# q, k and V of an attention block moved by DMA: transposes for q and k, a way through DRAM for V

## The reference

```python
U, _ = jnp.linalg.qr(P)                       # 288 x 64
R = expm(skew(silu(cond) @ W.T + b))          # 2 x 64 x 64
z = jnp.einsum('btn,nd->btd', x, U)
x = x + jnp.einsum('btd,nd->btn', jnp.einsum('btd,bde->bte', z, R) - z, U)
ada = jax.nn.silu(c) @ ada_w + ada_b          # shift, scale, gate, twice
def attention(x):
    qkv = (x @ qkv_w + qkv_b).reshape(n, t, 3, H, DH)
    q, k, v = qkv[:, :, 0], qkv[:, :, 1], qkv[:, :, 2]
    attn = jnp.einsum('nthd,ntkd->nthk', q * DH ** -0.5, k)   # of one token, head against head
    out = jnp.einsum('nthk,ntkd->nthd', jax.nn.softmax(attn, -1), v)
    return out.transpose(0, 2, 1, 3).reshape(n, t, d) @ proj_w + proj_b
x = x + gate_msa * attention(modulate(layernorm(x), shift_msa, scale_msa))
x = x + gate_mlp * (gelu(modulate(layernorm(x), shift_mlp, scale_mlp) @ fc1_w + fc1_b) @ fc2_w + fc2_b)
```

## Time and profile before

| | |
|---|---|
| median of 3 runs | 427.33 us (426.06 to 427.52) |
| profiled execution, first to last instruction | 422.3 us |
| median less that span | 5.0 us |
| busy TensorE | 397.1 us |
| busy VectorE | 291.1 us |
| busy ScalarE | 231.8 us |
| busy GpSimd | 115.9 us |
| mean granted TensorE clock, share of full | 0.987 |

### The profile page before, as it was taken

How to read it: one execution, slowest core, us unless ns; L and a number is a source line. 1 busy time by engine, 2 the same in 40 slices (tenths; PEclk the granted TensorE clock), 3 DMA queues, 4 the chain that set the end, 5 groups by cost and what they waited for, 6 DMA issues and landing times.

```text
span 422.3 us, 11278 instructions
## 1 busy us (share of the span) xinstructions
PE 397.1 (94%) x4547; PEld 256.5 (61%) x4547; DVE 291.1 (69%) x793; ACT 231.8 (55%) x485; POOL 115.9 (27%) x137
## 2 busy tenths in 40 slices
PE   8999999999989899899978898889999999999996
PEld 4656555666545566666646565558755566666675
DVE  2688875677689856667757766666899776746452
ACT  3356334433257899997786785665775342422100
POOL 5039999981008700000000000005420010101040
PEclk9999989999989999999999999999999999999999
DMA  6999000000000000000000000000000000000011
GB/s 166 305 316 271 24 4 2 12 7 2 2 0 2 2 2 3 2 2 5 2 4 3 5 4 4 4 2 2 0 2 1 16 28 16 23 20 16 29 43 42
DMA packets 7926, 14.68 MB, mean 35 GB/s; under 512 B 2555, under 2 KB 6239, under 8 KB 7748
## 3 DMA queue, kind: packets, MB, share of 16 engines
q1 hardware_dynamic: 7874, 13.96, 11.0%
HBM read 11.52 MB, written 2.38 MB: 33 GB/s over the span
## 4 chain that ended last, share of the span: by engine, by line
PE 71%; DVE 14%; ACT 10%; issue 4%; ACTq 0%; DVEq 0%
PE psum L957 13%; PE psum L973 13%; PE psum L517 9%; PE psum L803 6%; ACT scratch L1068 3%; PE psum L787 2%; PE psum L880 2%; PE psum L617 2%; DVE MX L1373 2%; ACT big L1101 2%; PE psum L934 2%; PE psum L629 2%; PE psum L751 2%; PE psum L573 2%; PE psum L608 2%
## 5 line engine op out<-in xcount | busy, mean ns | idle before, releaser
L957 PE MATMUL psum<-scratch,W 128*128 128x512 f16 (+1 forms) x252 | 57.9, 379 | 0.0
L973 PE MATMUL psum<-W,big 128*128 128x288 f16 x432 | 55.1, 286 | 0.0
L506 POOL TENSOR_TENSOR X<-X,big 128x288 f32<-128x288 f32 x16 | 13.0, 826 | 150.0 <-ACT big L1174 149.7
L803 PE MATMUL psum<-WQ,scratch 128*128 128x288 f16 (+1 forms) x336 | 50.5, 294 | 2.8 <-DVE scratch L1368 1.9
L1199 ACT ACTIVATE big<-psum 128x512 f32<-128x512 f32 x36 | 21.3, 597 | 57.3 <-PE psum L957 52.3
L973 PEld LDWEIGHTS psum<-W,big 128*128 128x128 f16 x432 | 42.2, 98 | 12.9
L1373 DVE TENSOR_REDUCE MX<-psum 128x8 f32<-128x1024 f32 x32 | 39.0, 1220 | 11.4 <-PE psum L751 11.0
L517 PE MATMUL psum<-ident 128*32 128x192 f32 (+3 forms) x142 | 43.8, 393 | 0.0
L1129 ACT ACTIVATE big<-psum 128x1024 f32<-128x1024 f32 x32 | 32.9, 1032 | 15.0 <-PE psum L843 14.7
L957 PEld LDWEIGHTS psum<-scratch,W 128*128 128x128 f16 (+1 forms) x252 | 24.6, 98 | 25.6
L803 PEld LDWEIGHTS psum<-WQ,scratch 128*128 128x128 f16 (+1 forms) x336 | 30.6, 100 | 14.8 <-DVE scratch L1368 2.4
(11 more groups left out here) (221 smaller groups left out, 770.5 us busy)
## 6 DMA issues: line engine op xcount, KB each, us to landing
X<-in_x_dram SPq DMA_DIRECT2D x4, 576.0 KB, 14.8
out_dram<-big SPq DMA_DIRECT2D x16, 144.0 KB, 1.7
big<-in_L_cond_W_dram SPq DMA_DIRECT2D x1, 2268.0 KB
big<-in_L_cond_ada_w_dram SPq DMA_DIRECT2D x2, 864.0 KB, 18.2
stage<-in_L_cond_fc_w_dram SPq DMA_DIRECT2D x1, 1296.0 KB, 18.9
big<-in_L_cond_fc_w_dram SPq DMA_DIRECT2D x1, 1152.0 KB
stage<-in_L_cond_qkv_w_dram SPq DMA_DIRECT2D x1, 864.0 KB
big<-in_L_cond_fc_w_dram SPq DMA_DIRECT2D x3, 144.0 KB
```

The costliest lines, as they stand in the source:

```text
L803: mm = pe.matmul(UB[gu % 2][:, 0:D], HT[0:r, n % 2, a_, P * a:P * a + P], WQ[0:r, w_, D * w:D * w + D], start=(p_ == 0), stop=(p_ == 6))
L957: mm = pe.matmul(FB[idx % 3], W1[0:r, w_, P * m:P * m + P], HT[0:r, n % 2, a_, :], start=(p_ == 0), stop=(p_ == 6))
L973: mm = pe.matmul(YB[t % 2][:, 0:D], g[:, a_, f, cols], W2[:, w_, f, :], start=(f == 0 and a_ + w_ == 0), stop=(f == NF - 1 and w_ == 1))
```

## The change

q and k are no longer turned on TensorE. SP issues one DMA transpose for each of q and k of a pair (16 in all), from `HQ`, which now holds two pairs with both tiles of a head side by side, into `QKT`. The columns come out in the order of tokens, so `operand` reads them with a step of 16. The row of maxima is no longer turned on TensorE either: ScalarE scales `MX` into `MRT`, and SP writes it with four DMAs. V goes from PSUM to `SV` by one ScalarE copy a tile, from there by SP into a DRAM tensor, and GpSimd's own queue reads it back in the form that `values` needs, with eight DMAs a pair, into one of six buffers. Buffers 0 to 3 lie in `big`, where `VT` was, 4 and 5 in `scratch`. GpSimd clears the buffers and sets their column of ones. The projections rotate through three banks in place of two.

```diff
+        values_d = nc.dram_tensor("value_rows", [2 * NCH, 8, 2, 16, D], F32, kind="Internal").ap()
...
-        UB, CB = [bank[2], bank[5]], [bank[6], bank[7]]
+        UB = [bank[2], bank[5], bank[6]]
...
         def operand(s_, c_, w, g, rows):
             b, u = divmod(s_, 16)
-            return QKT[b][R * c_:R * c_ + rows, w, P * (4 * u + g):P * (4 * u + g + 1)]
+            pr, v = divmod(4 * u + g, 16)
+            cols = QKT[b][R * c_:R * c_ + rows, w, 16 * P * pr:16 * P * (pr + 1)]
+            return cols.rearrange("p (t v) -> p v t", v=16)[:, v]
...
+            def store_values(pr, c_):
+                k = 2 * pr + c_
+                sp.wait_ge(v_copied, k + 1)
+                sp.dma_start(values_d[pr, :, c_], SV[:, k % 4, :]).then_inc(v_stored[k % 4], 16)
+
+            def turn_heads(pr, w):
+                if pr == NCH and w == 0:
+                    sp.wait_ge(x_rot, NT)
+                    sp.wait_ge(folded, 2 * B)
+                sp.wait_ge(qk_low, lows(6 * pr + 3 + w))
+                dst = QKT[pr // NCH][:, w, 16 * P * (pr % NCH):16 * P * (pr % NCH + 1)]
+                sp.dma_start_transpose(dst.rearrange("p (h t) -> p h t", h=H),
+                                       HQ[:, pr % 2, w].rearrange("p h e c -> p (h e c)")).then_inc(qk_in[pr], 16)
...
+            for pr in range(2 * NCH):
+                store_values(pr, 0)
+                turn_heads(pr, 0)
+                turn_heads(pr, 1)
+                store_values(pr, 1)
+                if pr == 6:
+                    max_row(0)
+            for n in range(1, 4):
                 max_row(n)
...
+            def spread_values(w):
+                for c_ in range(2):
+                    pool.wait_ge(v_stored[(2 * w + c_) % 4], 16 * (w // 2 + 1))
+                if w >= 6:
+                    pool.wait_ge(pv_ready, 4 * (w - 6) + 4)
+                for m in range(8):
+                    src = bass.AP(tensor=values_d.tensor, offset=values_d.offset + (2 * P * w + 32 * m) * D, ap=[[DH, H], [D, 32], [1, DH]])
+                    pool.dma_start(VGS[w % 6].rearrange("p (g d) -> p g d", d=32)[m:P:8, :, 0:DH], src).then_inc(v_in[w], 16)
...
+            pool.wait_ge(fill_done, FG + 1)
+            pool.memset(big[:, 8192:12288], 0.0).then_inc(vg_clear, 1)
...
+            for w in range(4):
+                spread_values(w)
+            pool.wait_ge(split_done, 3 * NCH)
+            pool.memset(scratch[:, 0:4 * CH], 0.0).then_inc(vg_clear, 1)
...
+            for w in range(4, 2 * NCH):
+                spread_values(w)
...
             def maxima(s_):
                 if s_ % 4 == 0:
-                    pe.wait_ge(col_done, JOB[(s_ // 4, 1, 3)] + 1)
+                    pe.wait_ge(qk_in[s_ // 4], 32)
...
             def values(s_):
                 if q == 0:
-                    pe.wait_ge(vg_ready, w + 1)
+                    pe.wait_ge(v_in[w], 128)
...
             def high(gu):
+                if w == 2:
+                    k = gu // 3
+                    if k >= 4:
+                        act.wait_ge(v_stored[k % 4], 16 * (k // 4))
+                    act.mul(SV[:, k % 4, :], UB[gu % 3][:, 0:D], 1.0 / (FINE * FINE)).then_inc(v_copied, 1)
+                    return
...
+                if pr >= 2:
+                    act.wait_ge(qk_in[pr - 2], 32)
```

More of the change, by code:

```diff
@@ L143, in build @@
         T32 = scratch[:, o:o + 2 * CH].rearrange("p (a n) -> p a n", a=2)
-        VG = scratch[:, 0:4 * CH].rearrange("p (a c g d) -> p a c g d", a=2, c=2, g=16)
+        VGS = [big[:, 8192 + 2 * CH * i:8192 + 2 * CH * (i + 1)] for i in range(4)] + [scratch[:, 2 * CH * i:2 * CH * (i + 1)] for i in range(2)]
+        VG = [v.rearrange("p (c g d) -> p c g d", c=2, g=16) for v in VGS]
         o += 2 * CH
@@ L201, in build @@
         att_const = sem("att_const")
-        col_ready, col_done = sem("col_ready"), sem("col_done")
-        vcol_ready, vcol_done = sem("vcol_ready"), sem("vcol_done")
-        mr_psum, mr_ready = sem("mr_psum"), sem("mr_ready")
+        qk_in = [sem(f"qk_in{i}") for i in range(2 * NCH)]
+        v_copied = sem("v_copied")
+        v_stored = [sem(f"v_stored{i}") for i in range(4)]
+        v_in = [sem(f"v_in{i}") for i in range(2 * NCH)]
+        mr_ready = sem("mr_ready")
         max_in = [sem(f"max_in{i}") for i in range(NCH)]
@@ L297, in build @@
         MROWS = HALVES + 8
[L298 to L307, removed]
         AHEAD = {24 + 3 * s_ // 2: s_ for s_ in range(16)}
         LATER = {st: 1 for st in range(16)}
-        ROWS_LATER, ROWS_BANK = {8: 2, 16: 3}, {8: VB[0], 16: MXB[0]}
+        ROWS_EARLY = {36: 0, 3 * 4 * NCH: 1}
+        ROWS_LATER = {8: 2, 16: 3}
         PAIRED = 18
@@ L314, in build @@
         EXP_TABLE_AT = 2 * NQ + 1
-        NSLOT = 6 * 2 * NCH + 7 + 4
-        assert max(slots) < NSLOT
+        NSLOT = NQ * NCH + 1
         def unit(gu):
@@ L381, in _ @@
             sp.dma_start(B2ALL, src).then_inc(in_b2, 16)
+            def store_values(pr, c_):
[10 more added lines that the diff above has]
+                                       HQ[:, pr % 2, w].rearrange("p h e c -> p (h e c)")).then_inc(qk_in[pr], 16)
             def max_row(n):
[L384 to L387, removed]
+                sp.wait_ge(mr_ready, n + 1)
                 for c_ in range(2):
[L389 to L393, removed]
+                    for k in range(2):
+                        at = 16 * P * (2 * (n % 2) + k)
+                        row = QKT[n // 2][R * c_ + MROWS:R * c_ + MROWS + 1, 0, at:at + 16 * P]
+                        sp.dma_start(row, MRT[:, n % 2, 32 * c_ + 16 * k:32 * c_ + 16 * k + 16]).then_inc(max_in[n], 16)
+            for pr in range(2 * NCH):
[6 more added lines that the diff above has]
+            for n in range(1, 4):
                 max_row(n)
@@ L485, in _ @@
                 pool.wait_ge(ht_ones, a_ + 1)
+            pool.wait_ge(fill_done, FG + 1)
+            pool.memset(big[:, 8192:12288], 0.0).then_inc(vg_clear, 1)
+            pool.wait_ge(vg_clear, 1)
+            pool.memset(big[:, 8192:12288].rearrange("p (g d) -> p g d", d=32)[:, :, DH:DH + 1], 1.0).then_inc(vg_clear, 1)
+            pool.wait_ge(vg_clear, 2)
             pool.wait_ge(in_wp, 96)
@@ L753, in maxima @@
                 mm.then_inc(mx_ready, 1)
[L755 to L789, removed]
             def qkv(gu):
@@ L822, in _ @@
                     qkv(gu)
-                for i in slots.get(gu, ()):
-                    job(i)
                 if gu in AHEAD:
@@ L1103, in _, with rows_out @@
+            def rows_out(n):
+                act.wait_ge(mx_used, 8 * (n + 1))
+                if n >= 2:
+                    act.wait_ge(max_in[n - 2], 64)
+                act.mul(MRT[:, n % 2, :], MX[:, n, :], 1.0 / MROW).then_inc(mr_ready, 1)
             for t in range(TPC):
@@ L1115, in _ @@
                     norm_root(1)
-                for i in slots.get(gu, ()):
-                    job_out(i)
+                if gu in ROWS_EARLY:
+                    rows_out(ROWS_EARLY[gu])
                 if GATE_AT <= gu < GATE_AT + 4:
@@ L1163, in _ @@
                         values_out(st // 4 - 1)
-                    if st % 4 < 2 and st // 4 + 1 == 4:
-                        for q in range(2 * (st % 4), 2 * (st % 4) + 2):
-                            v_late_out(st // 4 + 1, q)
-                if st % 4 == 3 and st // 4 + 1 < UNITS // 4:
-                    v_out(st // 4 + 1)
             def product_out(t):
@@ L1454, in normalise @@
                     dve.wait_ge(weights, 5)
+                    for pr in range(2 * NCH):
+                        dve.wait_ge(qk_in[pr], 32)
                 for c_ in range(2):
@@ L1483, in _ @@
                     values_out(st // 4 - 1)
-                if st % 4 < 2 and 4 < st // 4 + 1 < UNITS // 4:
-                    for q in range(2 * (st % 4), 2 * (st % 4) + 2):
-                        v_late_out(st // 4 + 1, q)
                 if st >= 4 and st % 4 == 2:
```

168 lines of the change are left out of this document (43 added, 125 removed).

## The result

The changed kernel takes 457.06 us at the median of four runs (447.53 to 465.21), the kernel before 427.29 us (426.06 to 427.52) beside it. The ratio is 1.054, 95% interval 1.0473 to 1.0608. The profiled execution is the one of 447.53 us: a span of 445.7 us. I forecast 467 us; slower was right, and nearly the size, but the cause that I named is wrong. A span lies 1.8 us under its time here, not 5.0: executions of the kernel before with 427.3 us have spans of 425.5 us, so the 422.3 us of the earlier trace rows are some 3 us short of a usual one.

What follows compares the result with a forecast made beforehand. The prediction took GpSimd's issuing of V's spread as the bound: time 302.5 + 8g, 462.5 us at g = 20, plus 4 us for low clock, forecast 467 us; range 427 to 543, 8 in 10 395 to 600.

Steps and rivals of the forecast that it cites:

- What is added to GpSimd: Spreading V rows by 64 DMAs on GpSimd's queue: 2.5 us each, 20 us a pair, called the deciding term.
- my low bound of 0.31: GpSimd's issue of one V DMA, priced like SP's tiny DMA: 0.31 us, 2.5 us a pair.
- g: GpSimd's time to issue one pair's eight V DMAs: forecast 20 us, high bound 41 us.
- My own threshold of 1.44 us a DMA: GpSimd's issue time per V DMA at which its bound equals the hidden case; g = 11.5 us.
- the hidden case: Rival: all transfers hidden behind other work; span 389 us, time 394, up to 415 with stepped reads; chance 0.20.
- What is added to TensorE: Scores and maxima read operands stepped by 16 elements: from nothing to a doubling, 21 us; 5 us taken.
- the gap that GpSimd leaves: TensorE's idle time while waiting for GpSimd's V rows, said to hold the 5 us of stepped reads.
- the idle clock: TensorE idle several us before each group of four steps, so its clock may fall; 4 us allowed.
- given back 3 us: Qkv stage: VectorE's 3.3 us close to TensorE's 3.5 per three slots, so 3 us deducted, leaving 23.
- T: Time of one 512 KB DMA transpose on SP: 4 us taken, bounds 1.7 and 13 us.
- The long wait on HQ: Rival: transposes set the pace, projections stall on HQ; T 7.3 to 13 us, 427 to 496 us; chance 0.20.
- the signs that I named: Profile afterwards: gapless GpSimd issues from 142 us, value-step waits, qkv end near 195 us, stepped groups near 0.33 us or double.

Runs made afterwards that it cites:

- step_before: Kernel before, with scores and maxima reading both operands at a step of 16 f16 elements; 475.0 and 475.9 us, median of four runs 479.1 us.
- before: The kernel before the change, unedited; 427.29 us at the median.
- after: The changed kernel, unedited; 457.06 us at the median of four runs, ratio 1.054 to the kernel before.
- flat_after: Changed kernel, with operands of scores and maxima read side by side again; 400.8 and 406.1 us, ratio 0.944.
- flat_split: flat_after with each of GpSimd's 64 DMAs cut into two of half the runs; 400.7 us, ratio 0.939.
- step8: Kernel before, both operands of scores and maxima read with a step of 8 elements (16 bytes), mask zero; 485.8 us, one run.
- step4: Kernel before, both operands of scores and maxima read with a step of 4 elements (8 bytes), mask zero; 457.5 us, one run.
- v_alone: Kernel before with only the V half of the change (V through DRAM, spread by GpSimd); q and k as before; 413.2 to 417.2 us, ratio 0.973.

## Why the prediction was right in number and wrong in cause

**The step that failed** is in "What is added to GpSimd": "This is the term that decides." I took 2.5 us a DMA, from two column steps of an elementwise add for each run of 72 bytes; the rows show 0.62 us, between my low bound of 0.31 and 2.5. With g = 4.95 the term vanishes: pair 7 was issued at 242.5, and its use, values(28), is at 295.2. My own threshold of 1.44 us a DMA said that the hidden case then holds. GpSimd's pace on tensor columns said nothing here of what a DMA costs it to issue.

**The second step that failed** stood in "What is added to TensorE": I took 5 us and a doubling as the high bound. It is 0.33 to 1.09 us for eight, over three times. 64 groups x 0.76 = 48.6 us. The pairs that differ in it alone give, by their shorter runs, 475.4 - 427.5 = 47.9 us (step_before and before) and 450.2 - 403.4 = 46.8 us (after and flat_after). By span they give 473.2 - 422.3 = 50.9 us and 445.7 - 406.4 = 39.3 us, where both profiled executions of the second pair have the early low clock; after against flat_split, which has less of it and differs in the doubled issues too, gives 445.7 - 398.9 = 46.8 us. So this term alone turns a gain of 24 us into a loss of 23. I had put it "inside the gap that GpSimd leaves"; there was no such gap. The bound was chosen, no row carried it, and it should have stood as a rival with its own price. That 467 us came near 457 is luck: by span the forecast held 72.5 us for GpSimd and the idle clock (461.5 - 389) that were not there, and in their place stood 46.8 us of steps and 9.9 us by which the hidden case was priced too low. The Trainium skill ("SBUF — State Buffer", in the section on Door 1) was right to warn of a step that leaves its 16-byte line each time, and step8 agrees: 413 ns against 220. By step4 it is too mild, since two elements a line already cost 291 ns; the measurement decides.

**The hidden case** was priced at a span of 389 us; flat_split shows 398.9. Attention: 10 us forecast, 64.3 - 57.2 = 7.1 found. Qkv stage: 23 forecast, 96.2 - 80.0 = 16.2 found. The missing 7 us are in part the stall at HQ (3.2 us at most in one wait in flat_split; on its chain of work that ended last two pieces of 7.79 and 6.75 us are transposes, before 162 us). The rest is a loop that I had not priced. That chain, in flat_split, from one group of maxima to the next but one:

```profile
181.33 0.40 PE psum L779 x8
181.72 1.84 PE psum L797 x14
183.59 0.66 ACT stage L1042
184.27 0.46 DVE stage L1339
184.73 1.14 DVE MX L1299
185.92 0.40 PE psum L779 x8
```

L797 are projections, L779 the maxima, L1042 the high half, L1339 the low half, L1299 the row maxima. Three slots take 4.59 us, where I had compared 3.5 us of TensorE with 3.3 of VectorE and given back 3 us in all: neither engine is full, the work passes from TensorE to ScalarE to VectorE and back, and TensorE stands 14.4 us for row maxima in all.

**The transposes.** T was forecast at 4 us. In the changed kernel the pairs start 8.0 and 7.9 us apart (146.37, 154.36, 162.27), so 4 us each in sequence; each lands 7.1 us after issue. The long wait on HQ that I described came once, 4.7 us on ScalarE and 4.2 on TensorE. The rule of the Trainium skill's page "Advanced Engine Details and Errata" (X-Bar Transpose), 350 to 400 GB/s, isn't borne out here: the DMA engines show a share of 0.98 in 145 to 205 us of the changed kernel while 152 GB/s move.

**The clock.** I foresaw low clock from idle time. It stayed low without any: in 213 to 264 us it is at 0.51 and TensorE busy 50.8 of 51.0 us. What it costs there, in work whose pace follows the clock: 14 sets of value matmuls at 1.02 in place of 0.58 us and three sets of output transposes (L859) at 1.97 in place of 1.09, 14 x 0.44 + 3 x 0.9 = 9 us. That is in the 46.8 us by which the two spans differ, not beside it, so the 48.6 us worked out from full-clock steps is no exact account: some of the longer groups probably fall into time in which TensorE stood idle before (it was busy 54.6 of 64 us of the attention stage), and the clock adds its share; no run separates the two.

**The rest.** GpSimd's queue did start at 144 us, but not without a gap, values(0) at 217.5 waited for nothing, and the qkv stage ended at 213.0 us (201.0 in flat_split), not near 195. Of the signs that I named, "double" for the stepped groups was the one to watch.

## What to carry to other kernels

Before a layout change, look at what the reader of the layout will do: here matmuls with a moving operand of f16 read 16 or 32 bytes apart took TensorE more than three times as long, and that ate twice what the rest of the change released. Steps of 4 bytes were free, and a stepped stationary operand cost little. A change of two halves deserves two runs: the V half alone wins 2.7%. A bound that no row carries must enter the range as a case of its own, not as a small allowance. And before the total of a single run is read, see whether the stages that the edit leaves alone are as long as before: 22 of step4's 30 us were not.

## What the hardware showed that was not expected

- The price of a stepped moving operand does not follow the clock: 1.09 us for eight at 2.4 GHz, 0.98 to 1.06 us at 1.2 GHz, while f32 value matmuls go from 0.58 to 1.02 us.
- TensorE's clock stayed near its lower level for 50 us and more while the trace has it busy 99% of the time, in each of the four kernels with a moving operand stepped by 16 or 32 bytes (after 0.51, step_before 0.54). At the start of the attention stage it also dips without such steps, but comes back within some 10 us: 0.83 in 220 to 230 us of before, 0.53 in 210 to 221 of v_alone. In step_before it stood at 1.00 in 190 to 230 us with TensorE busy 38.7 of 40, and fell behind that. Stepped operands are not needed for it either: in the first stage of step4 it is 0.59 in 45 to 115 us with TensorE busy 70.0 of 70. Why it fell is open.
- GpSimd issues a DMA of 512 runs of 72 bytes in 0.62 us and one of 256 runs in 0.55 us. The trace books 2048 packets of 1152 bytes for its 64 DMAs, not 32768, so sixteen runs share one.
- SP needs 2.4 to 3.7 us to issue one transpose of 512 KB in after. The DMA engines show a share of 0.98 at 152 GB/s there; in 160 to 170 us they move 188 GB/s at a share of 1.12, so the share is no exact measure of a limit.
